# Fill rows of the expert lists one block a step, block limits computed before the last image's hidden layer ends, class rows copied during the last block, and expert results stored half by half

## The reference

```python
h = token_mixer(x)                       # windowed exp-weighted average, projection, layernorm
h = concat([cls_tok, h])                 # 257 rows per image
h = h + gated_linear_recurrence(layernorm(h))
u = layernorm(h)
shared = gelu(u @ Wfc_s + bfc_s) @ Wproj_s + bproj_s
top 2 of softmax(u @ Wr)                 # 8 experts, gates renormalised
h = h + shared + sum over the 2 experts of gate * (gelu(u @ Wfc[e] + bfc[e]) @ Wproj[e] + bproj[e])
```

## Time and profile before

| | us |
|---|---|
| three runs | 982.44, 982.86, 985.98 (median 982.86) |
| the profiled execution, its own time | 984.09 |
| its span | 982.0 |
| TensorE busy | 921.2 (94%) |
| VectorE busy | 700.6 (71%) |
| ScalarE busy | 482.3 (49%) |
| GpSimd busy | 394.2 (40%) |
| moved by DMA | 89.11 MB |

### The profile page before, as it was taken

The page is one execution under the profiler, slowest core; times in us unless marked ns, Lnnn a source line. Parts: engine busy times, 40 slices in busy tenths (PEclk is TensorE's granted clock), DMA queues, the critical chain, the costliest instruction groups (busy, mean ns, idle before and its releaser), DMA issues.

```text
span 982.0 us, 21456 instructions
## 1 busy us (share of the span) xinstructions
PE 921.2 (94%) x6825; PEld 858.8 (87%) x6825; DVE 700.6 (71%) x2093; ACT 482.3 (49%) x1146; POOL 394.2 (40%) x475
## 2 busy tenths in 40 slices
PE   7887999999999999999995999999999999999995
PEld 5665988888888888887985999999999999999995
DVE  3578788999999999999886464645646565654643
ACT  2123455555455555454341555555555555555553
POOL 6442233444333444315553334343533434342322
PEclk9898899999999999999997999999999999999998
DMA  9600001111101111101662728282642827473222
GB/s 257 187 22 23 30 31 50 54 54 54 46 18 43 54 54 54 54 1 40 199 220 69 220 44 220 43 221 43 161 107 44 219 44 190 77 205 60 44 43 33
DMA packets 50536, 89.11 MB, mean 91 GB/s; under 512 B 6733, under 2 KB 31199, under 8 KB 50498
## 3 DMA queue, kind: packets, MB, share of 16 engines
q0 software_dynamic: 31440, 58.52, 24.8%
q1 hardware_dynamic: 19058, 30.11, 10.8%
HBM read 59.28 MB, written 29.09 MB: 90 GB/s over the span
## 4 chain that ended last, share of the span: by engine, by line
PE 36%; DVE 27%; issue 23%; POOL 9%; ACT 3%; POOLq 1%; DVEq 1%; DMA 0%; ACTq 0%; SPq 0%
PE ps_nd L810 11%; PE ps_proj L794 5%; POOL out L755 5%; DVE rden L1996 4%; PE ps_ri L794 3%; DVE GL L1810 3%; PE ps_ip L960 3%; PE ps_ip L794 3%; PE ps_h L975 3%; DVE w2l L2228 2%; DVE st L1827 2%; PE ps_proj L889 1%; PE ps_proj L891 1%; PE ps_proj L894 1%; DVE h L1833 1%
## 5 line engine op out<-in xcount | busy, mean ns | idle before, releaser
L1810 DVE TENSOR_TENSOR GL<-g_act,GH 128x256 fp32r<-128x256 f32 (+1 forms) x416 | 174.6, 426 | 168.1 <-ACT GH L1440 152.9
L810 PE MATMUL ps_nd<-w2h,GH 128*128 128x256 f32 x832 | 242.5, 291 | 6.1 <-DVE Y L1999 4.8
L1435 ACT ACTIVATE g_act<-ps_proj,fcb 128x256 f32<-128x256 f32 (+1 forms) x272 | 129.1, 475 | 234.9 <-PE ps_proj L794 226.3
L810 PE MATMUL ps_nd<-w2h,GL 128*128 128x256 f32 x832 | 234.2, 281 | 0.0
L810 PE MATMUL ps_nd<-w2l,GH 128*128 128x256 f32 x832 | 233.3, 280 | 0.0
L810 PEld LDWEIGHTS ps_nd<-w2h,GH 128*128 128x128 f32 x832 | 156.6, 188 | 12.2 <-DVE Y L1999 5.0
L1440 ACT CAST GH<-g_act 128x256 fp32r<-128x256 f32 (+1 forms) x416 | 161.3, 400 | 1.2
L810 PEld LDWEIGHTS ps_nd<-w2l,GH 128*128 128x128 f32 x832 | 157.4, 189 | 0.0
L810 PEld LDWEIGHTS ps_nd<-w2h,GL 128*128 128x128 f32 x832 | 156.7, 188 | 0.0
L794 PE MATMUL ps_proj<-xh,w1h 128*128 128x256 f32 (+1 forms) x544 | 122.6, 307 | 12.6 <-DVE E L1989 8.9
L755 POOL DMA_INDIRECT out<-yb,rows_to x72 | 115.5, 1605 | 16.8 <-issue 13.2
(11 more groups left out here) (281 smaller groups left out, 1932.1 us busy)
## 6 DMA issues: line engine op xcount, KB each, us to landing
R<-v_rows SPq DMA_DIRECT2D x37, 260.0 KB
w1h<-fc_w POOLq DMA_DIRECT2D x9, 1024.0 KB
w2h<-pj_w POOLq DMA_DIRECT2D x9, 1024.0 KB
stage<-fc_w POOLq DMA_DIRECT2D x9, 1024.0 KB
stage<-pj_w POOLq DMA_DIRECT2D x9, 1024.0 KB
x<-x SPq DMA_DIRECT2D x28, 256.0 KB, 4.0
v_rows<-tail_rows SPq DMA_DIRECT2D x8, 520.0 KB
out<-yb SPq DMA_DIRECT2D x16, 256.0 KB
```

What stands on the lines that cost most here:

```text
L810: last = pe.matmul(banks[a], g[:, j, a * P:(a + 1) * P], w[i][:, j, :], start=(j == 0 and q == 0), stop=(j == HT - 1 and q == 2))
L1435: act.activation(g_act[:, j % G_SLOTS, 0:width], banks[j % len(banks)][:, 0:width], ACT.Gelu_apprx_tanh, bias=fcb[i][:, j:j + 1]).then_inc ...
L1810: dve.tensor_tensor(GL[:, j, 0:width], g_act[:, j % G_SLOTS, 0:width], GH[:, j, 0:width].bitcast(F32), ALU.subtract).then_inc(gl_done, 1)
```

## The change

- `seconds` and `tails` go, with `ends_i` and the waits on their stores. Instead `fill(t)` writes block t of all eight lists in one store, for t = 0 to 16: 0 to 3 behind the load of image 3, 4 to 13 in the loop behind the load of each image, 14 to 16 behind the load of image 15. Each waits for the one before it. `rows_out` of image n waits for n + 2 fills.
- The limits (`block_bounds`) are computed right behind the last `slots_out`, before the last image's `GL` slices 1 to 7; the block places (`block_places`) before its `base_sum`.
- In a block, VectorE's bias and gate operations alternate by half, and GpSimd waits for and adds each half by itself.
- SyncE's class row copy waits for all blocks but the last, and no longer for the last R load; GpSimd itself waits for the last adds at its end.

```diff
-            def seconds(t, par):
...
-            def tails(t, par):
...
+            def fill(t, par):
+                if isinstance(t, int) and t == 0:
+                    sp.wait_ge(lines, 2)
+                after(sp, filled, 16 * t)
+                sp.dma_start(v_rows[0:DUMP, :].rearrange("(e l) m -> e l m", e=NE)
+                             [:, bass.ds(t * BLK, BLK), :].rearrange("e (p a) m -> p e a m", a=2),
+                             tail_rows[:].unsqueeze(1).to_broadcast([P, NE, 2, W])
+                             ).then_inc(filled, 16)
             def step(t, par):
                 x_in(t, par)
+                fill(t, par)
                 base_out(t, par)
...
-            sp.wait_ge(added, end * 32 + 32)
-            sp.wait_ge(rows_loaded, end * 16 + 16)
+            sp.wait_ge(added, end * 32)
...
             def rows_out(t, par):
-                    if isinstance(n, int) and n == 0:
-                        pool.wait_ge(seconds_stored, 16 * NE)
-                    if isinstance(n, int) and n == NIMG - 1:
-                        pool.wait_ge(tails_stored, 16 * NE)
+                    pool.wait_ge(filled, 16 * (n + 2))
                     pool_wait(pool, slots_ready, n + 1)
...
             def add_rows(b):
-                pool.wait_ge(carried, b * 2 + 1)
+                pool.wait_ge(carried, b * 3 + 1)
                 pool_wait(pool, added, b * 32 + 32).then_inc(carried, 1)
-                pool.wait_ge(carried, b * 2 + 2)
-                pool_wait(pool, y_done, b * 2 + (2 * SBLK + 2), "y").then_inc(carried, 1)
                 for a in range(2):
+                    pool.wait_ge(carried, b * 3 + (a + 2))
+                    pool_wait(pool, y_done, b * 2 + (2 * SBLK + a + 1), "y").then_inc(carried, 1)
                     pool.indirect_dma_start(
...
-            expert(NE, 0, *limits(NE), 0)
+            first, end = limits(NE)
+            expert(NE, 0, first, end, 0)
+            pool_wait(pool, added, end * 32 + 32).then_inc(carried, 1)
...
             gate_b(18, 0)
             slots_out(18, 0)
+            block_bounds(18, 0)
             low(18, 0, 1)
...
             low(18, 0, 7)
             u_low(18, 0)
             v_norm(18, 0)
+            block_places(18, 0)
             base_sum(18, 0)
...
                     dve.tensor_tensor(yt[:, a, :], y_loop[a], pjb[i][:], ALU.add
                                       ).then_inc(yt_done, 1)
-                dve.wait_ge(yt_done, b * 2 + 2)
-                for a in range(2):
+                    dve.wait_ge(yt_done, b * 2 + (a + 1))
                     dve.tensor_scalar(yb[:, a, :], yt[:, a, :], gate[:, a:a + 1], None, ALU.mult
                                       ).then_inc(y_done, 1)
```

More of the change, by code:

```diff
@@ L427, in step @@
                 x_in(t, par)
+                fill(t, par)
                 base_out(t, par)
             x_in(2, 0)
-            seconds(2, 0)
             x_in(3, 1)
+            fill(0, 0)
+            fill(1, 1)
+            fill(2, 0)
+            fill(3, 1)
             base_out(3, 1)
@@ L439, in mixer_sync @@
             x_in(15, 1)
+            fill(14, 0)
+            fill(15, 1)
+            fill(16, 0)
             base_out(15, 1)
@@ L2240, in constant, with count_chain, block_bounds, block_places @@
                 constants()
+            counted = [0]
+            def count_chain(instruction):
+                counted[0] += 1
+                instruction.then_inc(count_dve, 1)
+                dve.wait_ge(count_dve, counted[0])
+            def block_bounds(t, par):
+                chain = count_chain
+                dve.wait_ge(run_ready, NIMG + 1)
+                chain(dve.tensor_tensor(cnt["size"][:], run[:], list_f[:], ALU.subtract))
+                chain(dve.tensor_scalar(cnt_i[:], cnt["size"][:], float(BLK - 1), None, ALU.add))
+                chain(dve.tensor_scalar(cnt_s[:], cnt_i[:], BLK.bit_length() - 1, None,
+                                        ALU.arith_shift_right))
+                chain(dve.tensor_copy(cnt["n"][:], cnt_s[:]))
+                chain(dve.tensor_scalar(cnt["blocks"][:], cnt["n"][:], float(MIN_BLKS), None, ALU.max))
+                chain(dve.tensor_tensor_scan(cnt["end"][:], ones_pp[:, 0:NE], cnt["blocks"][:],
+                                             0.0, ALU.mult, ALU.add))
+                dve.memset(bounds[:, 0:1], 0)
+                dve.memset(lasts[:, 0:1], 0)
+                chain(dve.tensor_scalar(lasts[:, 1:NE + 1], cnt["end"][:], -1.0, None, ALU.add))
+                dve.tensor_copy(bounds[:, 1:NE + 1], cnt["end"][:]).then_inc(bounds_ready, 1)
+            def block_places(t, par):
+                chain = count_chain
+                dve.tensor_scalar(cnt["skip"][:], cnt["blocks"][:], -1.0, float(LIST_BLKS),
+                                  ALU.mult, ALU.add)
+                dve.tensor_copy(hop[:, NE - 1, :], block_f[:])
+                chain(dve.memset(carrier["count"][:], 0.0))
+                for e in range(NE - 1):
+                    last = dve.tensor_scalar(hop[:, e, :], block_f[:], cnt["end"][:, e:e + 1],
+                                             cnt["skip"][:, e:e + 1], ALU.is_ge, ALU.mult)
+                chain(last)
+                chain(dve.tensor_reduce(where[:], hop[:].rearrange("p e b -> p b e"), AX.X, ALU.add))
+                dve.tensor_copy(where_i[:], where[:]).then_inc(where_ready, 1)
             def cls_scan(t, par):
@@ L2514, in experts_vector @@
         def experts_vector(dve):
[L2515 to L2531, removed]
-                                         0.0, ALU.mult, ALU.add))
-            dve.memset(bounds[:, 0:1], 0)
-            dve.memset(lasts[:, 0:1], 0)
-            chain(dve.tensor_scalar(lasts[:, 1:NE + 1], cnt["end"][:], -1.0, None, ALU.add))
-            dve.tensor_copy(bounds[:, 1:NE + 1], cnt["end"][:]).then_inc(bounds_ready, 1)
-            dve.tensor_scalar(cnt["skip"][:], cnt["blocks"][:], -1.0, float(LIST_BLKS),
-                              ALU.mult, ALU.add)
-            dve.tensor_copy(hop[:, NE - 1, :], block_f[:])
-            chain(dve.memset(carrier["count"][:], 0.0))
-            for e in range(NE - 1):
-                last = dve.tensor_scalar(hop[:, e, :], block_f[:], cnt["end"][:, e:e + 1],
-                                         cnt["skip"][:, e:e + 1], ALU.is_ge, ALU.mult)
-            chain(last)
-            chain(dve.tensor_reduce(where[:], hop[:].rearrange("p e b -> p b e"), AX.X, ALU.add))
-            dve.tensor_copy(where_i[:], where[:]).then_inc(where_ready, 1)
             def next_info(b):
```

38 lines of the change are left out of this document (9 added, 29 removed).

## The result

The changed kernel takes 986.94 us (median of 20 runs, 984.39 to 991.15), the kernel before 983.05 beside it: ratio 1.0042, 95% interval 1.003 to 1.0054. That is 4 us slower. One of the 20 executions of the kernel before took 4655.41 us and stands outside of the ratio. The forecast was 981.7 in a range of 977.4 to 985.8: outside, and on the wrong side of no change.

A forecast was written before the change was run, and what follows sets the result against it. TensorE was taken as the bound (94% busy), with dips at the turn from mixer to experts and at the tail. Turn +0.9 and tail -2.1 gave -1.2: 982.86 to 981.7 us, range 977.4 to 985.8.

The forecast's parts named there:

- The block: Expert blocks: the same four VectorE operations in both orders, so nothing changes before the last block; costed at nothing.
- The tail: Behind the last block: halves -0.3, class row copy moved off the end -2.0, GpSimd's own marker +0.2; together -2.1 us.
- the second rival: At the end: GpSimd's drain sets the end even without the copy, so the tail gives 0.3 only: 983.5 us; chance 0.24.
- The turn: Mixer to experts: early limits and scatters, split holds slice 7, TensorE idles, clock loses 1.5; transposes 0.9 us later.
- the bound that I had left out of the sum: In the turn: slice 6 may be held by the split too, costing 0.7 us; kept as upper end only.
- The first block: 2.51 us from transposes to first block left unchanged; up to 2 us come back if shorter pauses keep the clock up.
- The fills: Seventeen stores, 36 MB instead of 6.4, on the queue of the x loads; x load is ahead, so costed at nothing.
- third rival: Mixer loop: x load slowed by sharing engines with the fill; 993 us if one microsecond late, 1,015 if three; chance 0.06.
- The sum: Turn +0.9 and tail -2.1 give -1.2 us on the span; execution's 1.2 above the median carried over: 981.7 us.

The follow-up runs named there:

- experiment 2: Changed kernel with VectorE scaling the two result halves in the old pairwise order, GpSimd's wait for each half kept: ratio 1.0001 to the kernel before.
- experiment 5: Changed kernel with the old pairwise order on VectorE only in the last block of every expert: ratio 1.0008 to the kernel before.
- experiment 7: Kernel before with only the class row copy moved into the last block and the last adds' wait put at VectorE's end: ratio 1.0002, tail 11.20 us.
- experiment 1: Changed kernel with the wait for the last two adds moved from GpSimd's end to VectorE's: ratio 1.003 to the kernel before, tail 10.27 us.
- experiment 6: Changed kernel with GpSimd's four quarter weight splits moved ahead of the scatters of images 14 and 15: ratio 1.0067 to the kernel before.
- experiment 3: Kernel before with only the dump rows' stores exchanged for the fills, one store a step: ratio 0.9999.
- experiment 10: Changed kernel with last wait on VectorE, halves pairwise, limits behind slices 1 to 7, GpSimd waiting for limits before its last two splits: ratio 0.9955 to kernel before.
- experiment 11: The kernel of experiment 10 with the block places moved behind the first low rows on VectorE: ratio 0.9945 to the kernel before, 979.31 us beside 984.59.
- experiment 4: Changed kernel with the block limits moved behind slices 1 to 7, just ahead of the block places: ratio 1.0017 to the kernel before.

## Why the prediction was wrong

**The block: the step that failed.** "Both orders have the same four VectorE operations, so nothing changes before the last block." Inside a loop that holds (12.01 us a block in both), and the four operations end only 0.16 us later than before. But the order has one wait more, and VectorE's sequencer stands in its last wait 0.39 us longer before it can leave the loop or go on to the register loads of the next expert; slice 0 of that expert comes the same 0.39 later. The first block of an expert is 0.32 to 0.42 longer at six of the seven changes and 0.16 at the seventh, together 2.45; the last block, entered by a loop's exit, is 0.13 to 0.17 longer at six and 0.10 at the seventh, together 1.04: that is the 3.55, but for rounding. I should have asked what is queued behind the added wait where the answer isn't simply the next block. Experiments 2 and 5 show that VectorE's order is the cause and where it costs; that it works through the sequencer's wait is read from the equal 0.39 in the timelines, and no run tests it by itself.

**The tail: mis-sized, -2.1 for +0.7.** The class copy was worth 0.2 (experiment 7), not 2.0, since GpSimd's drain ends with it: the second rival, given 0.24, was right. GpSimd's own wait, costed as a marker of 0.2, puts the landing ahead of the drain: 1.8 by experiment 1. On the good side the halves bring both adds forward by 0.8, where I had 0.6 and 0.3: the second add begins 1.86 us behind the first in either kernel (973.85 and 975.71; 973.17 and 975.03), so it comes forward with it and does not wait for its own half. Together -0.8, -0.2 and +1.8 give +0.8 for the +0.7 measured.

**The turn: right in mechanism.** Predicted were limits 3.6 us behind slice 0 (3.8 measured: 515.16 + 0.40 - 511.78), a split that begins at 521.2 to 521.5 on the old scale, 7.2 to 7.5 behind slice 0 (7.74), a held slice, and transposes 0.9 later than before: they are at 20.53 us behind slice 0 instead of 20.04, 0.5 later. The scatters started 0.8 us behind the slots, where 0.3 had been taken without a row for it. Inside that, two errors cancel. The register loads are 0.87 in the chain, not 3.50, because they no longer wait for the limits and begin beside the products. And the products behind the held slice, which start 0.4 later than forecast, took 2.93 + 3.96 us where 5.0 were forecast: slice 6 was held too (the bound that I had left out of the sum), and the lower clock lasted 5.3 us, where I had supposed three:

```profile
524.50:529.80 5.30, 5.26 (x24) 4.12 (x25) 4.58 (x17) 0.00 (x0) 0.00 (x0) 0.50 0.00 0
```

One reading in that part was loose: the `GL` of 1.36 us at 454.66 stood beside GpSimd's addition of a bias row (454.45 to 455.73), not beside a split.

**The first block: 1.2 us better than costed.** I had allowed for up to 2. TensorE's pause before the first transposes is 0.87 us instead of 8.44 (of which 3.50 were the loads):

```profile
534.04 1.11 PE L1382 MATMUL ps_t<-ident,R 128*128 128x128 f32 x4 [8.44 <-issue]
```
```profile
532.31 0.65 PE L1372 MATMUL ps_t<-ident,R 128*128 128x128 f32 x4 [0.87 <-issue]
```

And the granted clock over some 4 us around the first products is 1.00, the upper level (2.4 GHz), where it was 0.62, for most of it the lower one (1.2 GHz). Busy time by engine before, then after (stretch, its length, TensorE, its weight loads, VectorE, ScalarE, GpSimd, then clock, DMA share, GB/s):

```profile
537.00:541.00 4.00, 4.00 (x24) 4.00 (x24) 0.86 (x5) 1.69 (x5) 0.45 (x3) 0.62 0.15 19
```
```profile
534.00:538.00 4.00, 3.44 (x27) 3.34 (x28) 1.84 (x9) 2.19 (x6) 0.18 (x1) 1.00 0.02 6
```

The twelve products take 1.68 us instead of 2.93. In experiment 1, with a pause of 1.35, they take 2.43 and the block 13.08, so this gain is not there in every execution. The pause's length alone does not decide it: experiment 6 has 1.55, keeps a clock of 1.00 and a block of 11.70. What does stays open.

**The fills: right.** No x load is late (third rival, 0.06), and nothing ahead of the turn is slower (experiment 3).

**The sum.** -1.2 + 3.55 + 0.7 = +3.0 by the stages of the two profiles; with the turn and first block of experiments 1 and 5 (34.41 and 34.58 together, 0.3 under before), +4.0. Less the 0.45 outside of the span, which I had carried over as unchanged, that is +2.5 to +3.5. The ratio says +4.1, 2.9 to 5.3. How often the changed kernel's first block is the short one, and how often the long one, was not measured.

## What to carry to other kernels

An added wait costs nothing where the engine's next instruction is late anyway, and up to its full length where a loop's exit or register loads stand behind it; look at the loop's exits, not at its body. A wait for the last DMA belongs on an engine that has nothing else to do at its end, not on GpSimd, whose drain then starts after it. And if one long GpSimd operation stops VectorE, moving short work about only changes which instruction pays; what helped here (experiments 10 and 11) was to order the two so that the split starts when what stands next on VectorE is needed late.

## What the runs showed of the hardware that I had not expected

- GpSimd's drain behind indirect adds takes 3.75 us if they have landed before it (after, and experiments 2, 4, 5 and 6: 3751 to 3756 ns), and ends 4.2 to 4.5 us behind the end of the last issue if not.
- An instruction that VectorE has begun ahead of GpSimd's split is held by it: slice 6 in the changed kernel began at 518.91, 0.61 us before the split, where its like takes 0.43; the cast of experiment 4 began 0.56 before and its like takes 0.17. The Trainium skill, "SBUF — State Buffer", section "SBUF: two separate sides", calls the shared ports an exclusive lock that the first to start keeps for its instruction, and names as VectorE's candidates operations in a two-port mode or with two SBUF inputs. This case's traces agree with the lock: a VectorE instruction is held to the end of the split, or, in experiment 11, where VectorE got in between its two parts, to the end of a part (a sum of 1.97 us and a copy of 1.39). They don't agree with who gets it. The cast has one input only, so of the two candidates the two-port mode alone could cover it, and no run shows in which mode it ran. Two sums with one input in PSUM (`yb<-ps_nd,pjb`) took 0.76 us inside a split of the kernel before (509.49, the split from 508.78 to 513.52) and 0.77 outside of one (522.55). As the recorded starts are rough on GpSimd, the order in time may be off by some tenths; the held lengths are not.
- TensorE's register loads run ahead of its products if the value is there: with the limits early, as in the changed kernel and experiments 1, 2, 5 and 6, 3.50 us in the chain became 0.61 to 1.55.
